# A three-part decoder layer for 64 sequences: the order of the small steps between the attention steps is changed

## The reference

```python
x = x + self_attn(layernorm(x))            # 16 heads of 8: q,k,v, softmax(q k / sqrt(128)) v, @ Wff.T + bff
x = x + cross_attn(layernorm(x), ctx)      # 16 heads of 8, keys and values from ctx (77), mask, @ Wo.T + bo
x = x + experts(layernorm(x))              # below
...
proj = x @ Wp.T;  pn = proj / max(|proj|, eps)
gate_scores = pn @ sn.T / temperature      # 8 experts
top_v, top_i = top_k(gate_scores, 2);  gate_probs = softmax(top_v)
h  = gelu(x @ W1[e] + b1[e]);  eo = h @ W2[e] + b2[e]
out = sum over the two chosen experts of gate_probs * eo
```

## Time and profile before

| | before |
|---|---|
| median of 3 runs | 1185.13 us (1181.31 to 1186.98) |
| the profiled execution | 1185.62 us, span 1183.9 us |
| PE, PEld busy | 996.1 us (84%), 767.5 us (65%) |
| DVE, ACT, POOL busy | 749.3 us (63%), 799.0 us (67%), 593.3 us (50%) |
| mean DMA rate | 122 GB/s |

### The profile page before, as it was taken

How to read it: one execution, slowest core, us unless ns; L and a number is a source line. 1 busy time by engine, 2 the same in 40 slices (tenths; PEclk the granted TensorE clock), 3 DMA queues, 4 the chain that set the end, 5 groups by cost and what they waited for, 6 DMA issues and landing times. The chain is left out here.

```text
span 1183.9 us, 31785 instructions
## 1 busy us (share of the span) xinstructions
PE 996.1 (84%) x11621; PEld 767.5 (65%) x11621; DVE 749.3 (63%) x2074; ACT 799.0 (67%) x1649; POOL 593.3 (50%) x821
## 2 busy tenths in 40 slices
PE   2567889999999999999999999847529999999940
PEld 1345667777777777777777777635418888888830
DVE  2554746666667666676666674423258888888836
ACT  2144557777777777777777777635419999999930
POOL 4313423365655664664654643544534666666650
PEclk9997999999999999999999999978759999999975
DMA  3337684455455555545545642230452444232319
GB/s 92 83 75 157 141 187 102 120 142 146 128 151 134 134 136 140 142 126 140 151 112 147 147 110 73 57 81 31 136 161 76 125 129 113 79 83 75 84 56 372
DMA packets 120387, 144.16 MB, mean 122 GB/s; under 512 B 34189, under 2 KB 98528, under 8 KB 115432
## 3 DMA queue, kind: packets, MB, share of 16 engines
q1 hardware_dynamic: 108888, 120.33, 40.0%
q0 software_dynamic: 9168, 17.21, 4.8%
q10 hardware_dynamic: 2176, 4.59, 1.0%
HBM read 88.38 MB, written 55.36 MB: 121 GB/s over the span
## 5 line engine op out<-in xcount | busy, mean ns | idle before, releaser
L615 ACT ACTIVATE probs<-sc_a 77x512 f32<-77x512 f32 (+1 forms) x512 | 301.0, 592 | 148.5 <-PE sc_a L1008 93.2
L757 DVE TENSOR_REDUCE negm_m<-sc_m 128x4 f32<-128x512 f32 x256 | 169.5, 683 | 82.5 <-PE sc_m L987 81.4
L1305 POOL DMA_INDIRECT y_d<-yo,row x156 | 160.7, 1030 | 115.0 <-DVE yo L1419 73.6
L757 DVE TENSOR_REDUCE negm_cm<-sc_m 128x4 f32<-128x308 f32 x256 | 119.1, 471 | 144.5 <-PE sc_m L992 143.0
L477 POOL DMA_INDIRECT xs_d<-xrow,slot_i x128 | 131.9, 1031 | 121.3 <-PE sc_a L1008 80.0
L1022 PE MATMUL pv<-probs,big 128*32 128x128 f32 x4096 | 165.7, 280 | 0.6
L987 PE MATMUL sc_m<-ks,qs 96*128 96x128 bf16 x1024 | 105.3, 230 | 37.5 <-DMA ks<-stk_k 13.4
L1022 PEld LDWEIGHTS pv<-probs,big 128*32 128x32 f32 x4096 | 96.3, 109 | 56.2 <-ACT probs L615 28.6
L1400 DVE TENSOR_TENSOR gl<-g,gh 128x512 fp32r<-128x512 f32 x156 | 107.4, 689 | 35.1 <-ACT g L1349 34.6
L987 PEld LDWEIGHTS sc_m<-ks,qs 96*128 96x128 bf16 x1024 | 71.6, 102 | 82.6 <-issue 55.8
L1003 PE MATMUL sc_a<-cqs,cks 102*77 102x128 bf16 x1024 | 102.0, 223 | 4.9 <-DMA cqs<-cmscr 4.8
(11 more groups left out here) (202 smaller groups left out, 2333.7 us busy)
## 6 DMA issues: line engine op xcount, KB each, us to landing
xg<-xs_d SPq DMA_DIRECT2D x39, 260.0 KB
stk_q<-parts_q SPq DMA_DIRECT2D x16, 384.0 KB, 2.9
stk_k<-parts_k SPq DMA_DIRECT2D x16, 384.0 KB, 2.7
qs<-stk_q SPq DMA_DIRECT2D x16, 384.0 KB, 5.9
ks<-stk_k SPq DMA_DIRECT2D x32, 192.0 KB
stk_cq<-parts_cq SPq DMA_DIRECT2D x16, 384.0 KB, 2.9
cqs<-stk_cq SPq DMA_DIRECT2D x16, 384.0 KB
xin<-x_dram SPq DMA_DIRECT2D x16, 256.0 KB
```

Source lines behind the costliest of these rows:

```text
L615: nc.scalar.activation(probs[e % 4][0:rows], sc_a[e % 2][0:rows], ACT.Exp, scale=scale)\
L757: nc.vector.tensor_reduce(out=negm[n][:, s, HG * g + 4 * half:HG * g + 4 * half + 4], in_=sc_m[u % 2][:, 0:4 * cols].rearrange("p (j k) -> ...
L1305: nc.gpsimd.indirect_dma_start(out=y12_d, in_=yo[par][:, c, :], in_offset=None, bounds_check=2 * B * S - 1, oob_is_err=False, out_offset=b ...
```

## The change

Only step numbers change, and one helper is cut in two. In half x, TensorE's output projection of the cross-attention goes from step 5 to 6, the transposes of the normalised input from 8 to 9, of the context from 9 to 10, the products q, ck, k from 10, 11, 13 to 11, 12, 14. In half y, `project` goes from 5 to 6, the gate's two products from 8, 9 to 9, 10, the transposes of the second normalised block from 14 to 15, the count from 15 to 16, the product cq from 16 to 17. The copies on ScalarE and the sums, statistics and remainders on VectorE that follow them move by one step, mostly; the copy of the second block's transposes stays in step 15 and the v copy in 13. The statistics of the next input (`stats("1")`) go from step 10 to 5. `choose` is cut into `choose` (scores, the top values, their difference) and `point` (the indices), and `mark` goes from step 13 to 14.

```diff
@@ ScalarE, in_x and in_y
-                        if u == 8 and on_(t + 2):
+                        if u == 9 and on_(t + 2):
                             evac(xnT["1"][:], "x1T", t + 2, 0)
-                        if u == 9 and on_(t):
+                        if u == 10 and on_(t):
                             evac(cT[:], "cT", t, 1, TC)
-                        if u == 10 and on_(t + 2):
+                        if u == 11 and on_(t + 2):
                             first("q", t + 2)
-                        if u == 11 and on_(t):
+                        if u == 12 and on_(t):
                             wait_block(act, dumped["ck"], t - 1)
                             first("ck", t, bk_c)
-                        if u == 12 and on_(t + 2):
+                        if u == 13 and on_(t + 2):
                             second("q", t + 2)
-                        if u == 13 and on_(t + 2):
+                        if u == 14 and on_(t + 2):
                             first("k", t + 2)
-                        if u == 13 and on_(t):
+                        if u == 14 and on_(t):
                             second("ck", t)
...
-                        if u in (8, 9) and on_(t - 3):
-                            half = u - 8
+                        if u in (9, 10) and on_(t - 3):
+                            half = u - 9
...
-                        if 10 <= u < 10 + NS and on_(t):
-                            normalise("2", t, x2, u - 10)
+                        if 11 <= u < 11 + NS and on_(t):
+                            normalise("2", t, x2, u - 11)
@@ VectorE
                     nc.vector.tensor_tensor(out=dv[:], in0=top_v[:, :, 1], in1=top_v[:, :, 0], op=ALU.subtract)\
                         .then_inc(dv_ok.sem, 1)
+
+                def point(b):
+
                     for s in range(NS):
                         i = nc.vector.max_index(top_i[:, s, :], top_v[:, s, :], gs[:, s, :])
                     i.then_inc(gate_step.sem, 1)
@@ VectorE, in_x and in_y
-                        if u == 6 and on_(t - 3):
+                        if u == 7 and on_(t - 3):
                             wait_block(dve, x3_st, t - 4)
                             add_residual("c", t - 3, x2res[1 - par], x3)
-                        if u == 7 and on_(t - 3):
+                        if u == 8 and on_(t - 3):
                             stats("3", t - 3, x3)
-                        if u == 11 and on_(t + 2):
+                        if u == 12 and on_(t + 2):
                             wait_block(dve, part3["cq"], t - 1)
                             remainder("q", t + 2)
...
+                        if u == 5 and on_(t + 3):
+                            dve.wait_ge(x_in.sem, x_in.val(t + 3))
+                            stats("1", t + 3, xin)
-                        if u == 6 and on_(t):
+                        if u == 7 and on_(t):
                             wait_block(dve, x2res_ok, t - 1)
                             add_residual("s", t, xres, x2)
-                        if u == 7 and on_(t):
+                        if u == 8 and on_(t):
                             stats("2", t, x2)
-                        if u == 10 and on_(t + 3):
-                            dve.wait_ge(x_in.sem, x_in.val(t + 3))
-                            stats("1", t + 3, xin)
                         if u == 12 and on_(t - 3):
                             choose(t - 3)
                         if u == 13 and on_(t - 3):
+                            point(t - 3)
+                        if u == 14 and on_(t - 3):
                             mark(t - 3)
@@ TensorE, in_x and in_y
-                        if u == 5 and on_(t - 3):
+                        if u == 6 and on_(t - 3):
                             project("c", t - 3, cw_o)
...
-                        if u == 8 and on_(t + 2):
+                        if u == 9 and on_(t + 2):
                             pe.wait_ge(ln_ok["1"].sem, ln_ok["1"].val(t + 2))
                             transposes("x1T", t + 2, 0, [xn["1"][:, s, :] for s in range(NS)], 128)
...
-                        if u == 13 and on_(t + 2):
+                        if u == 14 and on_(t + 2):
                             product("k", t + 2, w_k[:], xnT["1"][:], T)
...
-                        if u == 14 and on_(t):
+                        if u == 15 and on_(t):
                             pe.wait_ge(ln_ok["2"].sem, ln_ok["2"].val(t))
                             transposes("x2T", t, 1, [xn["2"][:, s, :] for s in range(NS)], 128)
-                        if u == 15 and on_(t - 3):
+                        if u == 16 and on_(t - 3):
                             claim(0, "rank", t - 3)
...
-                        if u == 16 and on_(t):
+                        if u == 17 and on_(t):
                             pe.wait_ge(drained["x2T"].sem, drained["x2T"].val(t))
                             product("cq", t, cw_q[:], xnT["2"][:], T)
```

More of the change, by code:

```diff
@@ L851, in in_x @@
                             divide("c", t - 3, u)
-                        if u == 6 and on_(t - 3):
+                        if u == 7 and on_(t - 3):
                             wait_block(dve, x3_st, t - 4)
                             add_residual("c", t - 3, x2res[1 - par], x3)
-                        if u == 7 and on_(t - 3):
+                        if u == 8 and on_(t - 3):
                             stats("3", t - 3, x3)
-                        if u == 11 and on_(t + 2):
+                        if u == 12 and on_(t + 2):
                             wait_block(dve, part3["cq"], t - 1)
                             remainder("q", t + 2)
-                        if u == 12 and on_(t):
+                        if u == 13 and on_(t):
                             wait_block(dve, part3["ck"], t - 1)
                             remainder("ck", t, bk_c)
-                        if u == 14 and on_(t + 2):
+                        if u == 15 and on_(t + 2):
                             wait_block(dve, part3["k"], t + 1)
@@ L1102, in in_y @@
                             transposes("x3T", t - 3, 0, [xrow[(t - 3) % 2][:, s, 0, 0:D] for s in range(NS)], 128)
-                        if u == 5 and on_(t):
+                        if u == 6 and on_(t):
                             project("s", t, w_ff)
```

## The result

The changed kernel takes **1215.22 us** (median of 4 runs, 1212.0 to 1217.32) against 1184.51 for the kernel before on the same chip (1181.31 to 1186.98): a ratio of 1.0269, interval 1.0234 to 1.0303. It is slower, as forecast, by 31 us where 20 were forecast; the time lies inside the range. The profiled execution took 1217.32 us.

The account below looks back on a forecast made before the run. TensorE, busy 194.99 of 200 us, was taken to bound the kernel. Terms -5.6 + 14 x 0.4 + 14 x 0.5 + 12 x 0.5 + 12 x 0.5 + 1 = +20 gave 1205 us, range 1187 to 1218.

Parts of the forecast that it names:

- The two waits removed: TensorE's input transposes waiting on `parts_m` and product cq on its operand's copy: 0.4 us a block won, 5.6 us.
- Maxima in half x: Half x, scores of unit 11 wait for VectorE's maximum 9 behind the sum's statistics: 0.4 us a block lost.
- End of half x: Product k one step later, last values wait for ScalarE's copies and exponentials: 0.5 us a block lost.
- the fast rival: ScalarE and VectorE have hidden slack, so only the two removed waits count: 1180 us, chance 0.10.
- the sign that the prediction named: End of half x: copies of k and ck done before the last shifted scores end would decide for the fast rival.
- End of half y: Second block's last quarter queues behind the v copy and an exponential, its transposes wait: 0.5 us in 12 blocks.
- The gate: `stats("2")` ends about 1.2 us later, VectorE waits about 2 us for GpSimd's root; costed at nothing.
- The load of `xin`: Half y, VectorE waits for the load behind maximum 5, delaying unit 8's scores: 0.5 us in 12 blocks, ends 0 and 1.6.
- The late-load rival: Every `xin` load takes 5.9 us: 2.2 us a block, 26 us instead of 6, 1225 us; chance 0.14.
- Filling: First half y with work: statistics of `xin` go ahead of the residual sum, +1 us once.
- Only the waits go away: The fast rival's name in the prediction: 1180 us, chance 0.10.
- gain and loss cancel: Only the maxima term and half the load term remain: 1188 us; chance 0.18, mixed cases included.

Follow-up runs that it names:

- the last experiment: Kernel before with four small moves in half x, plus half x's divisions and the transposes behind them one step later: 1179.21 us, ratio 0.9972 to the kernel before.

## Why the prediction was right, and where its sizes were off

*The two waits removed* (-0.4 a block): both are gone, and the transposes of the input start on time. Right.

*Maxima in half x* (+0.4): 0.4 by the starts, and moving only the statistics gives 0.40 back. Right, with the unit and the maximum that the prediction named.

*End of half x* (+0.5): 0.42, given back exactly by moving only k. Right. The slack on ScalarE that the fast rival needed was not there. But the sign that the prediction named for that rival was misread. It said that the copies of k and ck end 1.3 us after the last shifted scores; in the trace before, the copy of ck ends at 525.65 and the last shifted scores run from 525.86 to 526.59:

```profile
525.20 0.45 ACT L597 ACTIVATE parts_ck<-rest_ck 128x308 bf16<-128x308 f32 x1
525.86 0.73 PE L1003 MATMUL sc_a<-qs,ks 102*128 102x128 bf16 x8
```

So the copies were done in time before the change, and by its own sign the rival should have won. What decided was the new place: there the product starts one step later, the last shifted scores run from 593.50 to 594.11, and the copies end at 594.42, behind them.

*End of half y* (+0.5): 0.44, and 0.48 come back with the v copy moved. Right. The rival cause, a late root on GpSimd, is ruled out by that run, which moved only the copy.

*The gate* (nothing): VectorE waits 1.61 for the root, near the 2 forecast, and no TensorE row waits for it. Right.

*The load of `xin`* (+6 in all): the term that was mis-sized. It is 13 us. The two ends for the load's duration were well chosen: in the ten steady blocks VectorE starts on it 3.46 to 6.64 us after the issue, where 3.54 and 5.9 were the ends. What failed was to take one value near the low end and multiply it by twelve. The load has no usual duration: of twelve full halves y, the last of which has no load, seven pay nothing, three 0.1 to 1.3, and two 3.4 and 4.1. Nor has its issue a usual time: it comes 2.32 to 5.25 after the start of the half, where the working had 3.6 for all. Issue and duration together say which half is late: up to 7.9 nothing is lost, 8.2 costs 0.07, 9.2 costs 1.0, 9.5 costs 1.3 (a load of only 4.22, issued at 5.25), 10.0 and 10.7 cost 3.4 and 4.1. And the price of the two longest was too low, since 1.7 of each is the clock that falls behind the wait, which the working did not have. The late-load rival, 26 us of it and always, is wrong too. The Trainium skill's fit (DMA: Bandwidth & Descriptors, Anatomy of one DMA), an estimate of 2.6 us for these bytes, lies below the shortest load measured here, 3.46. That section gives the fit for DMAs issued by GpSimd, and this load is issued by SyncE among other traffic, so the trace does not test it; it was right not to use it here.

*Filling* (+1): 6.1 up to the second half y. With the statistics back in step 10 this is 1.6, and the two halves behind it lose another 1.3 there; so the load costs 9.9 + 4.5 - 1.3 = 13.1, the 13 above, and 2.9 are left for the early part. They hold the other terms in the halves not yet counted, and perhaps the clock; they were not taken apart.

*A term that was missing*: the projection's product costs more at its new place, 0.14 in half x and 0.20 in half y, an estimated 5 us in all. In half y the product `w_ff` started 0.89 ahead of the next group; now it stands between the values and the transposes of `third_m`, and it is 1.09:

```profile
557.32 1.16 PE L982 MATMUL wb<-w_ff,onT 128*128 128x128 f32 x8
558.41 0.40 PE L1051 MATMUL wb<-identb,third_m 128*48 128x128 bf16 x4
```

Moved back, the 0.20 come back. With this term the halves close: -0.30 + 0.40 + 0.42 + 0.14 = 0.66 of the 0.69 in half x, and -0.10 + 0.44 + 0.20 = 0.54 of the 0.57 in half y. The claim "the amount of work stays the same, so each term is a wait" was the wrong step here: a group takes a little more or less by what stands beside it. Which neighbour it is stays open; the product `cw_v`, which has 77 rows and stands behind values in both kernels, takes 0.93 to the scores behind it.

With the measured sizes: steady halves 14.6, load 13.1, early part 2.9, behind the last half y 1.1, in all the profiled run's 31.7. The forecast was 11 us short: 7 by the load, and the rest mostly by the projection's place and the early part. "Only the waits go away" and "gain and loss cancel" are ruled out: each of the four terms came back when its piece alone was moved.

What stays open: why one load takes 6.6 us and another 4.1 at the same place of the program; how much of the early part is the clock; what the 1.1 behind the last half y is; and why the last experiment's first half y is 3.1 longer.

## What to carry to other kernels

A piece of work is not only something that waits; while it runs on the bounding engine it is the time in which other engines catch up. Before moving a piece away from a wait, ask who used its time: here the maxima at its old place, and the copies' distance to the end of the half, cost more than the wait. Two of the experiments missed for the same reason, and a third in part. Moving a wait for a load earlier needs the longest arrival, not the usual one, and often it is the issue that should move. Read starts on the bounding engine rather than noted waits; equal stages repeat to 0.01 us, and each edit shows as its own number in them.

## What the runs showed of the hardware

TensorE's clock fell inside the busy part of the program after short waits. In the changed kernel the scores at 654.49 waited 2.35, and the granted clock was 0.99 in the stretch up to 655.00 and 0.50, the lower level, from there to 658.30; after a wait of 1.70 at 371.25 it was 0.50 from 371.60 to 375.00. In the kernel with only the input's statistics moved it fell four times, after waits of 1.84 to 3.04. It does not follow from a wait's length alone: in the kernel with the v copy moved the scores at 280.11 waited 2.65, and the clock was 1.00 from 280.20 to 287.00. In the kernels without a late load it did not fall once between 180 and 700 us. In the changed kernel it added 1.7 us to each of the two waits; with the projections back, a half y with a noted wait of 3.76 was 6.76 too long, and the granted clock was 0.51 from 274.00 to 280.70.

The same 256 KB load from the same line of the program was ready for VectorE between 3.46 and 6.64 us after its issue, in ten blocks that do the same work.
